# An audio block of mixer, mLSTM and eight experts on one core: a shorter router and last norm, and one expert pair of each of nine output blocks stored ahead

## The chip, the cores and the metric

The kernel runs on one core of one Trainium2 chip. The metric is the device time of one execution in microseconds (us), lower being better. All arithmetic is in float32.

## The reference

`x` is [64, 4, 256] and the output [64, 256, 64] (batch, token, feature). Three sub-blocks follow one another:

```python
# token mixer: 8 rounds in both directions, then a combination
a = x^T W1 + b1;  up = down = 0
for _ in range(8):
    up   = relu(a + shift_r(up) @ W2.T + b2)
    down = relu(a + shift_l(down) @ W2.T + b2)
h = relu(x^T W3 + b3 + shift_r(up) @ W4.T + b4 + shift_l(down) @ W4.T + b4)
# gated recurrence over 256 tokens (mLSTM) on layernorm(h), then an RMS norm
h = h + rmsnorm(mlstm(layernorm(h))) * norm_scale
# eight experts on z = layernorm(h), weighted per token
feat = mean(z, axis=0)                       # over the 64 batch elements
w = softmax(feat @ Wr + br)                  # [256, 8]
e = relu(bn(z @ W1[e] + b1)); e = relu(bn(e @ W2[e] + b2)); y = e @ Wo[e] + bo
out = h + sum_e w[:, e] * y[:, :, e]
```

The router's weights `w` depend on the mean over all batch elements, so no expert output can be weighted before the last batch element has been normalised. The first two layers of an expert don't depend on `w`.

## The kernel before, in words

The 64 batch elements are eight groups of eight. A half of a group is a tile of 128 partitions by 512 columns (two batch elements of 64 features on the partitions, two more side by side in the columns). `turn(it, ...)` exists on every engine and runs three stages of different groups interleaved by hand: the mixer of group `it`, the recurrence of group `it - 1` (`att`), and the `late` part of group `it - 2`: the RMS norm, the update of `HH` (the residual stream), and the norm whose result is kept in `XN2`. Turns 0 to 7 have a mixer; turn 8 has the recurrence of group 7 and the late part of group 6; turn 9 has only the late part of group 7. Engines work through their own lists in order and meet at semaphores.

The late part in turn 9: ACT squares `HR` (L538), PE averages (`same_half`, L781), DVE adds (L1212), ACT takes logarithm and exponential (L596, L600), POOL multiplies (`RSL`, L414), DVE updates `HH` (L1246), PE centres (`center`, L774), ACT squares (L617), PE averages (L951), ACT takes logarithm and exponential (L634, L637), DVE multiplies into `XN2` (L1297), POOL adds four slices of it into `feat` (L434).

Work ahead: `ahead_step(i)` computes the first two layers of expert pair `i` before the router is known. The experts are four pairs (EP = 4), and the activations 16 output blocks `F` of 512 columns (512 x 128), so there are 64 tasks `t`, with block `t // 4` and pair `t % 4`. Seven tasks, t = 0 to 6, are stored in `H2_AHEAD`: steps 0 to 4 in turn 8, 5 and 6 in turn 9, and the second layer of task 6 behind it. PE does `experts_in` (L848) and `experts_mid` (L856), ACT both activations (L487, L493).

Behind turn 9, DVE works out whether the decays are out of range (`wide_f`, L1363 to L1374), with a PE transpose between (L1023), and sets `wide_ready`. Then every engine reads this flag (`plain_pass`, L260: `value_load` at L263) and jumps past a long alternative pass that these inputs don't need.

The router: PE multiplies `feat` by `wr` and adds `br_row` (L1035, L1036); DVE and ACT make the softmax (L1380 to L1388); DVE spreads each weight over 64 columns (`wb`, L1391); PE turns this with 16 matmul records into the weight planes (L1043), and transposes `wn` (L1047); DVE copies the planes into `WM[0]` (L1394), ACT and DVE make the half-swapped `WM[1]` (L688, L1399). `bias_out` (L1051) makes the experts' bias per token, which DVE copies to `BOW` (L1433).

The expert stream: PE's loop (L1089) issues for each `t` the first layer of `t` (`l1`), the second layer of `t - 1` (`l2`) and the third of `t - 2` (`l3`, L1079). ACT does the first activation (L694), DVE the second one together with the weight (`weigh`, L1412). Stored tasks are weighed from SBUF, others from PSUM. The four third layers of a block add up in QB0 and QB1; then DVE adds the residual (`finish`, L1420, L1422) from the tile that POOL made (L462), transposes it (`token_major`, L1427), and SP stores it (L335). DVE's order is t = 0, 1, 2, ..., with `finish` behind the first weighing of the next block, and `token_major` behind the second. The next block's first third layer (`l3` with p = 0) waits for `finish` (semaphore `res`).

Of the kernel before, what the change touches and what calls it, by code (L numbers as in the profile page):

```python
# [42 lines left out]
def build(nc, x, tok_W1, tok_b1, tok_W2, tok_b2, tok_W3, tok_b3, tok_W4, tok_b4, Wq, bq, Wk, bk, Wv, bv,  # L43
          Wg, bg, input_bias, norm_scale, Wr, br, W1, b1, g1, be1, m1, v1, W2, b2, g2, be2, m2, v2, Wo, bo, out):
    with ExitStack() as ctx:
# [26 lines left out]
        col2 = sb("col2", [P, 8])  # L72
        bn_s = sb("bn_s", [P, 2, EP])
# [37 lines left out]
        V0 = sb("V0", [P, HC])  # L111
        UT0 = sb("UT0", [P, HC])
# [14 lines left out]
        bn_rows = SQL[0:NBN, P:2 * P]  # L127
        w2_raw = RSL[:, 0:P]
# [13 lines left out]
        wb = NN[:, :].rearrange("p (t c) -> p t c", t=2)  # L142
        wn = M[:, 0:16].rearrange("p (t e) -> p t e", t=2)
        wx = M[:, 16:32].rearrange("p (t e) -> p t e", t=2)
        wmx, wsm, wrc = M[:, 32:34], M[:, 34:36], M[:, 36:38]
        wt = Q[0:E, 0:T]
# [6 lines left out]
        QB = [ctx.enter_context(nc.psum_tensor(f"QB{j}", [P, 512], F32)) for j in range(4)]  # L153
# [33 lines left out]
        def bn_cols(name):  # L187
# [45 lines left out]
            "lg_mm", "mx", "nmx", "ex", "rc", "wn", "wb", "w_mm", "w_out", "wt_mm", "wt_out", "bo_mm", "bo_out",  # L233
            "ws_out", "l1_mm", "h1", "l2_mm", "h2", "hw", "l3_mm", "res_a", "res", "tr_out")}
        stored = [sem("b_stored0"), sem("b_stored1")]
# [6 lines left out]
        range_max, range_mm, range_all, wide_ready = (sem(n) for n in ("range_max", "range_mm", "range_all", "wide_ready"))  # L242
        feat_cleared, fold_mm, range_parts = sem("feat_cleared"), sem("fold_mm"), sem("range_parts")
# [6 lines left out]
        def settle(engine, it, mix, att, late):  # L250

            if mix:
                engine.wait_ge(s["feat_out"], SB * it)
            if att:
                engine.wait_ge(s["h1_a"], it)
                engine.wait_ge(s["h1_v"], it)
            if late:
                engine.wait_ge(s["hr_out"], 2 * it - 2)

        def plain_pass(engine, turn, prepare=None, again=None):  # L260
# [3 lines left out]
            with engine.If(wide != 0):  # L264
# [6 lines left out]
                engine.wait_ge(s["feat_out"], 2 * SB * G)  # L271
# [4 lines left out]
        N_AHEAD = 2 * EP - 1  # L276
# [12 lines left out]
        def _(sp):  # L289
# [34 lines left out]
            with sp.If(wide != 0):  # L324
                with sp.Fori(0, G) as g:
# [5 lines left out]
            with sp.Fori(0, G) as g:  # L331
                for f in range(2):
                    sp.wait_ge(b["tr_out"], 2 * g + f + 1)
                    for q in range(4):
                        sp.dma_start(ov[bass.ds(g, 1), q // 2, q % 2, f].rearrange("a i n b j -> (a i) n b j"),  # L335
                                     OUTT[f][32 * q:32 * q + 32, :].rearrange("i (n b j) -> i n b j", n=2, j=32))\
                            .then_inc(stored[f], 16)
            for f in range(2):
                sp.wait_ge(stored[f], 64 * G)

        @block.gpsimd
        def _(pool):
# [63 lines left out]
            def turn(it, att, late, plain=False):  # L406
                a, l = it - 1, it - 2
                gl = l - G if plain else l
                if plain:
                    settle(pool, it, False, att, late)  # L410
                if late:
# [18 lines left out]
                if late:  # L430
                    for n in range(SB):
                        pool.wait_ge(s["xn2_out"], 2 * l + n // 2 + 1)
                        pool.wait_ge(s["feat_out"], SB * l + n)
# [7 lines left out]
            turn(G + 1, False, True)  # L441
# [5 lines left out]
            def clear_feat():  # L447
                pool.wait_ge(s["feat_out"], SB * G)
# [5 lines left out]
                pool.wait_ge(feat_cleared, 4)  # L454

            plain_pass(pool, plain_turn, clear_feat)

# [8 lines left out]
        def _(act):  # L466
# [15 lines left out]
            def ahead_step(i, done=0):  # L482

                if i < N_AHEAD:
                    for k in range(2):
                        act.wait_ge(ahead["l1_mm"], 2 * (done + i) + k + 1)
                        nc.scalar.activation(H1[i % 2][:, k, :], TB[k][:, :], ACT.Relu,  # L487
                                             bias=bn_t[:, 0, i % EP:i % EP + 1]).then_inc(ahead["h1"], 1)
                if i > 0:
                    j = i - 1  # L490
                    for k in range(2):
                        act.wait_ge(ahead["l2_mm"], 2 * (done + j) + k + 1)
# [976 lines left out]
```

## Time and profile before

| | us |
|---|---|
| median of three timed runs | 651.35 |
| lowest, highest | 648.98, 654.53 |
| the profiled execution, whole | 656.66 |
| its span in the trace | 654.9 |
| its mean granted TensorE clock | 0.95 |
| busy in the span: PE, DVE, ACT, POOL | 594.1, 438.4, 343.4, 128.8 |

The profile is of one execution. PE is the TensorE matmul, PEld its weight load, DVE VectorE, ACT ScalarE, POOL GpSimd, SP SyncE. A granted clock of 1.00 is 2.4 GHz, 0.50 is 1.2 GHz. Matmul durations of one instruction overlap, since four matmuls of 64 by 64 go side by side; start-to-start times and the chain give the pace. L12 is line 12 of the kernel before.

### The profile page before, as it was taken

Reading aid. Unit: us, or ns where it says so; the run is one execution under the profiler, and the core shown is the slowest. Engines: PE = TensorE matmul, PEld = TensorE weight load, DVE = VectorE, ACT = ScalarE, POOL = GpSimd, SP = SyncE. Lnnn points to the kernel's source line nnn. Section 1 sums busy time; section 2 is a strip of 40 time slices with the busy share of each in tenths; the row PEclk is TensorE's granted clock in tenths of the full one; section 3 lists DMA queues with packets and bytes.
Section 4 is the critical chain, followed back from the end, with each engine's and each line's share of the span. In section 5 each row is a group of like instructions: output and inputs, shape, how many; then the busy total and the mean of one; then the engine's idle time right before and its main releaser. Section 6 shows DMA issues by size and latency. Waiting matters only on the chain.

```text
span 654.9 us, 11761 instructions
## 1 busy us (share of the span) xinstructions
PE 594.1 (91%) x4715; PEld 231.9 (35%) x4715; DVE 438.4 (67%) x742; ACT 343.4 (52%) x609; POOL 128.8 (20%) x145
## 2 busy tenths in 40 slices
PE   7889898999999999999999999786479999999995
PEld 5233342344334334334334334342323333333331
DVE  2335864893895895894795794782277767676765
ACT  1237352854845845845845846965213444444441
POOL 9100020132113113113113113242220101010100
PEclk8999996989999999989999989997579999999998
DMA  1300000000000000000000000000002121212122
GB/s 41 87 3 2 1 3 0 1 2 3 2 1 3 2 1 4 0 2 5 1 0 2 1 1 2 0 1 1 6 2 33 17 33 17 35 18 33 17 33 33
DMA packets 37433, 7.29 MB, mean 11 GB/s; under 512 B 36405, under 2 KB 36701, under 8 KB 37373
## 3 DMA queue, kind: packets, MB, share of 16 engines
q1 hardware_dynamic: 36301, 5.72, 5.1%
q8 instruction: 40, 0.66, 0.4%
q0 software_dynamic: 768, 0.69, 0.4%
q14 instruction: 20, 0.16, 0.1%
q10 hardware_dynamic: 304, 0.07, 0.0%
HBM read 2.26 MB, written 4.19 MB: 10 GB/s over the span
## 4 chain that ended last, share of the span: by engine, by line
PE 73%; DVE 18%; issue 4%; ACT 3%; POOL 1%; POOLq 0%; DVEq 0%
PE TB L731 14%; PE TB L721 9%; PE QB L1079 7%; PE QB L754 6%; PE TB L848 6%; PE QB L781 5%; PE TB L856 4%; DVE M L1241 3%; PE QB L774 3%; PE TB L829 3%; PE QB L856 2%; PE TB L781 2%; DVE E L1412 2%; PE QB L798 2%; DVE XC_IS L1422 2%
## 5 line engine op out<-in xcount | busy, mean ns | idle before, releaser
L479 ACT ACTIVATE U<-TB 128x512 f32<-128x512 f32 x128 | 69.5, 596 | 135.1 <-PE TB L721 135.1
L731 PE MATMUL TB<-U,w2T 64*64 64x512 f32 x896 | 130.4, 618 | 8.6 <-ACT U L479 4.7
L694 ACT ACTIVATE E<-TB,bn_t 128x512 f32<-128x512 f32 x114 | 72.1, 683 | 95.5 <-PE TB L848 95.5
L1123 DVE TENSOR_SCALAR U<-TB 128x512 f32<-128x512 f32 x128 | 82.0, 683 | 57.5 <-PE TB L721 57.5
L721 PE MATMUL TB<-X,w_in 6*128 6x512 f32 x512 | 74.0, 648 | 2.1 <-DVE fw L1355 0.9
L848 PE MATMUL TB<-XN,fw 64*64 64x512 f32 x512 | 69.6, 605 | 1.2 <-DVE AT L1394 0.9
L731 PEld LDWEIGHTS TB<-U,w2T 64*64 64x64 f32 x896 | 43.8, 136 | 67.1 <-issue 30.1
L1079 PE MATMUL QB<-E,fwo 64*64 64x512 f32 x240 | 63.2, 598 | 4.1 <-DVE XC_IS L1422 3.5
L1079 PE MATMUL QB<-E,fwo_sw 64*64 64x512 f32 x240 | 62.4, 598 | 0.0
L1412 DVE SCALAR_TENSOR_TENSOR E<-TB,t_neg,AT 128x512 f32<-128x512 f32 x56 | 39.5, 747 | 29.8 <-PE TB L856 29.8
L754 PE MATMUL QB<-XC_IS,wproj 64*64 64x512 f32 x384 | 56.5, 606 | 2.9 <-ACT LI L582 2.7
L414 POOL TENSOR_TENSOR RSL<-HR,RSL 128x512 f32<-128x512 f32 x16 | 20.9, 1328 | 179.6 <-ACT RSL L600 179.6
L1412 DVE SCALAR_TENSOR_TENSOR E<-QB,t_neg,AT 128x512 f32<-128x512 f32 x58 | 40.7, 744 | 16.9 <-PE QB L856 16.9
L462 POOL TENSOR_TENSOR SQ<-HH,LF_UT 128x512 f32<-128x512 f32 x16 | 21.2, 1329 | 146.3 <-DVE XC_IS L1420 126.5
L422 POOL TENSOR_TENSOR IK<-NN,M 128x512 f32<-128x512 f32 x16 | 20.1, 1275 | 147.5 <-DVE NN L1278 147.5
L856 PE MATMUL TB<-E,fw 64*64 64x512 f32 x280 | 39.1, 615 | 0.2 <-ACT E L493 0.2
L774 PE MATMUL QB<-HH,center_mat 64*64 64x512 f32 x128 | 25.6, 749 | 14.8 <-DVE AT L1129 9.7
L721 PEld LDWEIGHTS TB<-X,w_in 6*128 6x128 f32 x512 | 20.2, 185 | 51.4 <-issue 48.2
L848 PEld LDWEIGHTS TB<-XN,fw 64*64 64x64 f32 x512 | 20.0, 135 | 36.3 <-ACT E L694 25.7
L798 PEld LDWEIGHTS QB<-Q,K 64*128 64x128 f32 x256 | 23.2, 198 | 26.2 <-issue 13.4
L798 PE MATMUL QB<-Q,K 64*128 64x256 f32 (+1 forms) x256 | 29.2, 359 | 3.1 <-DVE AT L1129 3.1
L1079 PEld LDWEIGHTS QB<-E,fwo 64*64 64x64 f32 x240 | 16.7, 134 | 42.6 <-issue 24.6
(218 smaller groups left out, 918.7 us busy)
## 6 DMA issues: line engine op xcount, KB each, us to landing
result<-V SPq DMA_DIRECT2D x64, 64.0 KB, 1.8
X<-in_x SPq DMA_DIRECT2D x32, 8.0 KB
XN<-in_ffn_v SPq DMA_DIRECT2D x2, 256.0 KB, 4.3
XN<-in_ffn_g SPq DMA_DIRECT2D x2, 256.0 KB, 4.7
fw<-in_ffn_W POOLq DMA_DIRECT2D x2, 128.0 KB, 2.9
fw<-in_ffn_W POOLq DMA_DIRECT2D x2, 64.0 KB, 2.6
fwo<-in_ffn_Wo POOLq DMA_DIRECT2D x2, 64.0 KB, 2.3
fwo_sw<-in_ffn_Wo POOLq DMA_DIRECT2D x2, 64.0 KB, 2.3
```

The costliest lines, as they stand in the source:

```text
L479: nc.scalar.activation(U3[:, 2 * j:2 * j + 2, 1:T + 1], rowsof(TB[j][:, :]), ACT.Relu)\
L694: nc.scalar.activation(H1[t % 2][:, k, :], TB[k][:, :], ACT.Relu, bias=bn_t[:, 0, t % EP:t % EP + 1]).then_inc(b["h1"], 1)
L721: pe.matmul(TB[j][:, :], w_in[32 * j:32 * j + KA, 0:P], X[32 * j:32 * j + KA, buf, :], start=(k == 0), stop=True).then_inc(s["mix_mm"], 1)
L731: pe.matmul(TB[j][half[r ^ (j % 2)], :], w2T[half[r], D * r:D * r + D], U3[half[r], 2 * j:2 * j + 2, 2 * down:2 * down + T], start=True, s ...
L754: mm = pe.matmul(bank[half[r ^ h], :], wproj[half[r], PROJ[p], :], XC_IS[half[r], hs(h)], start=True, stop=True)
L781: mm = pe.matmul(bank[half[r], :], mat[half[r], D * r:D * r + D], src[half[r], :], start=True, stop=True)
L798: mm = pe.matmul(bank[:, T * c:T * c + w], K[half[k], f:f + C], Q[half[k], f:f + w], start=True, stop=True)
L848: mm = pe.matmul(banks[k][half[e], :], fw1[half[r], t % EP, D * e:D * e + D], XN2[half[r], HC * F:HC * F + HC], start=True, stop=True)
L856: mm = pe.matmul(banks[k][half[e ^ k], :], fw2[half[e], t % EP, D * e:D * e + D], H1[t % 2][half[e], k, :], start=True, stop=True)
L1079: mm = pe.matmul(QB[r][half[k], :], (fwo, fwo_sw)[k][half[r], p, :], src[half[r], k, :], start=(p == 0), stop=(p == EP - 1))
L1123: nc.vector.tensor_scalar(U3[:, 2 * j:2 * j + 2, 1:T + 1], rowsof(TB[j][:, :]), 0.0, None, ALU.max)\
L1412: nc.vector.scalar_tensor_tensor(out=rowsof(v[:, k, :]), in0=rowsof(bank[k] if bank else v[:, k, :]), scalar=t2_neg[:, k, t % EP:t % EP + ...
```

## The change

- *Which tasks are stored.* `stored` is now t = 0, 4, 8, ..., 32, the first pair of each of nine blocks: eight by `ahead_step` (N_AHEAD = 8) and the ninth, t = 32, "parked": its layers are issued on PE around the logits, and ACT stores it. Their buffers are others (`X`, both parts of `U`, `K`, `NC_`, `LI`, `decay0` and so on). `made` lists the tasks whose layers run in the stream, with t = 32 first.
- *Who stores.* ACT does the second activation for stored tasks 0 to 5 and 7, DVE for task 6 (`ON_DVE` = 6). In turn 9, pair 5 keeps its place, pair 6 goes before the third list of projections (behind `rms_mm`), pair 7 to the place that pair 6 had, and the last second layer behind turn 9 as before.
- *Late part of turn 9.* The products of L414 move from POOL to DVE. The last multiplies into `XN2` move behind `plain_pass` on DVE. POOL's four last adds into `feat` are left out; PE adds group 7 in the logits instead, four slices by `wr`, two matmuls each.
- *Range check.* `range_parted` moves into turn 8 on DVE, the transpose to PE's start of turn 9, the rest to DVE's turn 9 ahead of the products.
- *Router.* One instruction for both token halves; no spreading over 64 columns. `wn` is written four times, 32 columns apart, so that two transposes put the weights at partitions 0, 32, 64, 96, and eight matmuls with a constant `pick` matrix (8 rows each) make all planes of `WM`, half-swapped ones included. DVE and ACT copy half of the planes each.
- *Order.* `weigh_order` weighs a stored t > 0 before t - 1. In PE's loop a stored task's third layer is issued directly ahead of its successor's. `finish` and `token_major` come one weighing later where the block's first task is stored.

The core of the diff ("..." where lines are left out):

```diff
-        H2_AHEAD = [E3[:, :], E2[:, 1024:2048], U[:, 0:1024], K[:, :], H2_4[:, :], RS_FS[:, :], E2[:, 0:1024]]
+        H2_AHEAD = [E3[:, :], H2_4[:, :], X[:, :, :].rearrange("p a c -> p (a c)"), U[:, 0:PC], U[:, PC:2 * PC], K[:, :],
+                    NC_[:, :], LI[:, :], decay0[:, :, :].rearrange("p n t -> p (n t)"), IK[:, :], V0_UT0[:, :], EO[:, :]]
         H2_AHEAD = [v.rearrange("p (s c) -> p s c", s=2) for v in H2_AHEAD]
         WM = [AT[:, 0:4, 0:T], AT[:, 4:8, 0:T]]
+        WM_BY_PAIR = AT[:, :, 0:T].rearrange("p (v j) c -> p j v c", v=2)
...
-        N_AHEAD = 2 * EP - 1
+        N_AHEAD, N_PARKED, ON_DVE = 8, 1, 6
+        stored = [EP * i for i in range(N_AHEAD + N_PARKED)]
+        stored_in = {t: H2_AHEAD[i] for i, t in enumerate(stored)}
+        made = stored[N_AHEAD:] + [t for t in range(2 * EP * G) if t not in stored_in]
+        weigh_order = sorted(range(2 * EP * G), key=lambda t: t - 1.5 if t in stored_in and t > 0 else t)
+        weighed = {t: 2 * i + 2 for i, t in enumerate(weigh_order)}
...
-                if late:
+                if late and not last_late:
...
-                if late:
+                if late and gl < G - 1:
...
+            h1(0)
+            act.wait_ge(b["nmx"], 1)
+            nc.scalar.activation(wx, wx, ACT.Exp).then_inc(b["ex"], 1)
+
+            park(0)
+            h1(1)
+            act.wait_ge(b["w_mm"], 1)
+            nc.scalar.activation(WM_BY_PAIR[:, 2:4], QBALL[:, 1024:2048].rearrange("p (j v c) -> p j v c", j=2, v=2),
+                                 ACT.Identity).then_inc(b["ws_out"], 1)
+
+            for i in range(N_PARKED + 1, len(made)):
+                h1(i)
...
                 if last_late:
+                    pe.wait_ge(range_max, 1)
+                    pe.wait_ge(s["den_sq"], 2 * G - 1)
+                    pe.transpose(QB[0][0:1, 0:P], wide_f[:, 0:1], ident[:, :]).then_inc(range_mm, 1)
...
-            l1(N_AHEAD)
+            l1(0)
+            pe.wait_ge(s["feat_out"], SB * (G - 1))
+            pe.wait_ge(wide_ready, 1)
+            pe.wait_ge(s["den_sq"], 2 * G)
+            for t in range(2):
+                pe.matmul(QB[t][:, 0:E], ones_row[:, :], br_row[:, :], start=True, stop=False)
+                pe.matmul(QB[t][:, 0:E], feat[:, P * t:P * t + P], wr[:, :], start=False, stop=False)
+            for n in range(SB):
+                pe.wait_ge(b["xn2_last"], n // 2 + 1)
+                for t in range(2):
+                    o = (G - 1) * PC + T * n + P * t
+                    mm = pe.matmul(QB[t][:, 0:E], XN2[:, o:o + P], wr[:, :], start=False, stop=(n == SB - 1))
+                    if n == SB - 1:
+                        mm.then_inc(b["lg_mm"], 1)
+            l2(0)
+
+            pe.wait_ge(b["wn"], 1)
+            for t in range(2):
+                mm = pe.transpose(QB[3][:, P * t:P * t + P], wn[:, t, :, :].rearrange("p j r -> p (j r)"), ident[:, :])
+            mm.then_inc(b["wt_mm"], 1)
+            l1(1)
+            pe.wait_ge(b["wt_out"], 1)
+            pe.wait_ge(pick_ready, 5)
+            for v in range(2):
+                for j in range(EP):
+                    mm = pe.matmul(QB[j][:, T * v:T * v + T], pick[32 * j:32 * j + E, D * v:D * v + P], wt[32 * j:32 * j + E, :],
+                                   start=True, stop=True)
+            mm.then_inc(b["w_mm"], 1)
+
+            l2(1)
+            l1(2)
             bias_out()
-            for t in range(N_AHEAD - 1):
+            n = len(made)
+            for i in range(N_PARKED + 2, n + 2):
+                if i < n:
+                    l1(i)
+                if i - 1 < n:
+                    l2(i - 1)
+                t = made[i - 2]
+                if t - 1 in stored_in:
+                    l3(t - 1)
                 l3(t)
...
+                if last_late:
+                    for e in range(2):
+                        nc.vector.tensor_reduce(pick_col[:, e:e + 1], ident[:, e:e + 103:34], AX_X, ALU.add).then_inc(pick_ready, 1)
+                    dve.wait_ge(pick_ready, 2)
+                    for i in range(3):
+                        nc.vector.tensor_copy(pick[:, D * i:D * i + D], pick_col[:, i % 2:i % 2 + 1].to_broadcast([P, D]))\
+                            .then_inc(pick_ready, 1)
+                    range_check()
+                    for h in range(2):
+                        dve.wait_ge(s["rr_out"], 2 * l + h + 1)
+                        nc.vector.tensor_tensor(RSL[:, hs(h)], HR[:, hs(h)], RSL[:, hs(h)], ALU.mult).then_inc(s["y_out"], 1)
...
+            for h in range(2):
+                dve.wait_ge(s["rs2_out"], 2 * G - 1 + h)
+                nc.vector.tensor_tensor(xn2(G - 1, h), hh(G - 1, h), RSL[:, hs(h)], ALU.mult).then_inc(b["xn2_last"], 1)
+            dve.wait_ge(b["wn_cleared"], 1)
+            lg = QBALL[:, 0:1024].rearrange("p (t c) -> p t c", t=2)[:, :, 0:E]
+            dve.wait_ge(b["lg_mm"], 2)
+            nc.vector.tensor_reduce(wmx, lg, AX_X, ALU.max).then_inc(b["mx"], 1)
+            dve.wait_ge(b["mx"], 1)
+            nc.vector.tensor_tensor(wx, lg, wmx.unsqueeze(2).to_broadcast([P, 2, E]), ALU.subtract).then_inc(b["nmx"], 1)
+            dve.wait_ge(b["ex"], 1)
+            nc.vector.tensor_reduce(wsm, wx, AX_X, ALU.add).then_inc(b["sm"], 1)
+            dve.wait_ge(b["sm"], 1)
             nc.vector.reciprocal(wrc, wsm).then_inc(b["rc"], 1)
             dve.wait_ge(b["rc"], 1)
-            for t in range(2):
-                nc.vector.tensor_scalar(wn[:, t, :], wx[:, t, :], wrc[:, t:t + 1], None, ALU.mult)\
-                    .then_inc(b["wn"], 1)
-            for t in range(2):
-                dve.wait_ge(b["wn"], t + 1)
-                nc.vector.tensor_copy(wb[:, t, :].rearrange("p (e c) -> p e c", c=D),
-                                      wn[:, t, :].unsqueeze(2).to_broadcast([P, E, D])).then_inc(b["wb"], 1)
+            nc.vector.tensor_tensor(wn[:, :, :, 0:E], wx.unsqueeze(2).to_broadcast([P, 2, EP, E]),
+                                    wrc.unsqueeze(2).unsqueeze(3).to_broadcast([P, 2, EP, E]), ALU.mult).then_inc(b["wn"], 1)
+            dve.wait_ge(b["wt_mm"], 1)
+            nc.vector.tensor_copy(wt, QB[3][:, 0:T]).then_inc(b["wt_out"], 1)
...
-            for t in range(2 * EP):
+            for t in weigh_order:
+                if t == 2:
+                    dve.wait_ge(b["ws_out"], 1)
                 weigh(t)
-                if t == 1:
+                if t == 0:
                     dve.wait_ge(b["bo_mm"], 1)
                     nc.vector.tensor_copy(BOW, QB[3][:, 0:T]).then_inc(b["bo_out"], 1)
-                if t == EP:
-                    finish(0)
-                if t == EP + 1:
-                    token_major(0)
-            for t in range(2 * EP, 2 * EP * G):
-                weigh(t)
-                if t % EP == 0:
-                    finish(t // EP - 1)
-                if t % EP == 1:
-                    token_major(t // EP - 1)
+                F, behind = t // EP - 1, t % EP - (t - t % EP in stored_in)
+                if F >= 0 and behind == 0:
+                    finish(F)
+                if F >= 0 and behind == 1:
+                    token_major(F)
```

`bias_out`, `l1`, `l2` and `l3` do what they did. `l2` for the second task of `made` beyond the parked one waits for `bo_out`, since it writes the bank of the bias.

## Rows read from the trace of the kernel before

**Rows 1.** The page, busy time and share of the span.

```profile
PE 594.1 (91%) x4715; PEld 231.9 (35%) x4715; DVE 438.4 (67%) x742; ACT 343.4 (52%) x609; POOL 128.8 (20%) x145
```

**Rows 2.** Stretches: from:to, length, busy by engine (instructions), PEclk, DMA share, GB/s.

```profile
120.00:390.00 270.00, 261.24 (x2091) 104.53 (x2085) 209.53 (x353) 168.49 (x309) 58.43 (x53) 0.98 0.01 2
...
455.00:470.00 15.00, 7.00 (x35) 3.30 (x27) 2.80 (x12) 6.21 (x14) 3.27 (x4) 0.61 0.02 6
470.00:480.00 10.00, 7.95 (x30) 5.05 (x31) 6.12 (x12) 2.41 (x4) 0.00 (x0) 0.50 0.01 2
480.00:490.00 10.00, 7.38 (x40) 2.92 (x38) 6.93 (x9) 0.00 (x0) 3.39 (x2) 0.82 0.00 0
```

**Rows 3.** The chain that ended last, hand-over: start, length, what.

```profile
447.94 1.27 POOL RSL L414
...
449.24 1.74 DVE HH L1246
...
451.03 2.63 PE QB L774 x8
...
459.40 0.70 DVE XN L1297
...
463.89 3.02 issue
466.90 0.56 PE QB L1035 x2
...
469.08 0.18 DVE M L1380
...
471.16 3.77 PE TB L1043 x16
...
474.95 1.24 DVE AT L1394
```

**Rows 4.** The same chain from the first layer to the last transpose.

```profile
476.23 1.99 PE TB L848 x8
...
479.37 3.73 PE QB L1056 x8
...
501.46 1.09 PE QB L1079 x8
502.55 0.86 PE TB L848 x8
...
512.24 1.09 PE QB L1079 x8
...
641.56 1.09 PE QB L1079 x8
...
650.19 0.71 DVE V L1427
```

**Rows 5.** PE's sequencer at line 263, the flag: durations in ns, start in us.

```profile
L263 PEldq TENSOR_LOAD <-wide_i x1: 492/492/492, 462.3 to 462.3; - x1
...
L263 PEldq SEQ_ASSERT  x1: 24/24/24, 463.1 to 463.1; - x1
```

**Rows 6.** Stretches of 2 us, columns as in rows 2 (granted clock third from last).

```profile
446.00:448.00 2.00, 0.00 (x0) 0.00 (x0) 0.68 (x1) 1.87 (x5) 0.06 (x1) 1.00 0.00 0
450.00:452.00 2.00, 0.97 (x6) 0.60 (x10) 1.64 (x2) 0.00 (x0) 0.43 (x1) 0.50 0.00 0
456.00:458.00 2.00, 1.58 (x14) 0.49 (x6) 0.00 (x0) 2.00 (x5) 0.00 (x0) 0.94 0.00 0
458.00:460.00 2.00, 0.00 (x0) 0.00 (x0) 0.60 (x1) 1.89 (x4) 0.00 (x0) 0.92 0.00 0
482.00:484.00 2.00, 2.00 (x11) 0.79 (x13) 0.89 (x2) 0.00 (x0) 0.38 (x1) 0.61 0.00 0
```

**Rows 7.** Groups of the weighing, from SBUF (beside POOL) and from PSUM.

```profile
L1412 DVE SCALAR_TENSOR_TENSOR K<-K,t_neg,AT 128x512 f32<-128x512 f32 x2 | 2.4, 1248 | 0.0
...
L1412 DVE SCALAR_TENSOR_TENSOR E<-TB,t_neg,AT 128x512 f32<-128x512 f32 x56 | 39.5, 747 | 29.8 <-PE TB L856 29.8
```

More of the change, by code:

```diff
@@ L408, in turn @@
                 gl = l - G if plain else l
+                last_late = it == G + 1 and not plain
                 if plain:
                     settle(pool, it, False, att, late)
-                if late:
+                if late and not last_late:
                     for h in range(2):
@@ L480, in relu, with ahead_h1, ahead_h2, ahead_again @@
                         .then_inc(s["relu_a"], 1)
-            def ahead_step(i, done=0):
-                if i < N_AHEAD:
[L485 to L492, printed above, removed]
-                        nc.scalar.activation(H2_AHEAD[j][:, k, :], TB[2 + k][:, :], ACT.Relu,
-                                             bias=t2_pos[:, k, j % EP:j % EP + 1]).then_inc(ahead["h2"], 1)
+            def ahead_h1(i, done=0):
+                p = stored[i] % EP
+                for k in range(2):
+                    act.wait_ge(ahead["l1_mm"], 2 * (done + i) + k + 1)
+                    nc.scalar.activation(H1[i % 2][:, k, :], TB[k][:, :], ACT.Relu,
+                                         bias=bn_t[:, 0, p:p + 1]).then_inc(ahead["h1"], 1)
+            def ahead_h2(i, done=0):
+                p = stored[i] % EP
+                for k in range(2):
+                    act.wait_ge(ahead["l2_mm"], 2 * (done + i) + k + 1)
+                    nc.scalar.activation(H2_AHEAD[i][:, k, :], TB[2 + k][:, :], ACT.Relu,
+                                         bias=t2_pos[:, k, p:p + 1]).then_inc(ahead["h2"], 1)
+            def ahead_again(i, done):
+                if i < N_AHEAD:
+                    ahead_h1(i, done)
+                if 0 < i <= ON_DVE or i == N_AHEAD:
+                    ahead_h2(i - 1, done)
             def att_plain(a, g):
@@ L851, in experts_in, with experts_mid @@
                             mm.then_inc(done, 1)
-            def experts_mid(t, banks, done):
+            def experts_mid(t, hidden, banks, done):
                 for k in range(2):
@@ L856, in experts_mid @@
                         mm = pe.matmul(banks[k][half[e ^ k], :], fw2[half[e], t % EP, D * e:D * e + D],
-                                       H1[t % 2][half[e], k, :], start=True, stop=True)
+                                       hidden[half[e], k, :], start=True, stop=True)
                     mm.then_inc(done, 1)
@@ L863, in ahead_step @@
                     after(pe, ahead["h1"], 2 * (done + i))
-                    experts_in(i, TB[0:2], ahead["l1_mm"])
+                    experts_in(stored[i], TB[0:2], ahead["l1_mm"])
                 if i > 0:
@@ L1124, in relu, with ahead_h2, ahead_again @@
                         .then_inc(s["relu_v"], 1)
+            def ahead_h2(i, done=0):
+                p = stored[i] % EP
+                for k in range(2):
+                    dve.wait_ge(ahead["l2_mm"], 2 * (done + i) + k + 1)
+                    nc.vector.tensor_scalar(H2_AHEAD[i][:, k, :], TB[2 + k][:, :], t2_pos[:, k, p:p + 1], 0.0, ALU.add, ALU.max)\
+                        .then_inc(ahead["h2"], 1)
+            def ahead_again(i, done):
+                if ON_DVE < i < N_AHEAD:
+                    ahead_h2(i - 1, done)
             def scores(a, bs):
@@ L1184, in turn @@
                 gm, ga, gl = (it - G, a - G, l - G) if plain else (it, a, l)
+                last = it == G and not plain
+                last_late = it == G + 1 and not plain
                 if plain:
@@ L1293, in turn @@
                     relu(it, 7)
-                if late:
+                if late and gl < G - 1:
                     for h in range(2):
@@ L1297, in turn @@
                         nc.vector.tensor_tensor(xn2(gl, h), hh(gl, h), RSL[:, hs(h)], ALU.mult).then_inc(s["xn2_out"], 1)
+                if last_late:
+                    dve.wait_ge(s["lam_out"], G)
+                    for i in range(6, N_AHEAD - 1):
+                        ahead_h2(i)
+                if last:
+                    range_parted()
                 if mix:
```

223 lines of the change are left out of this document (108 added, 115 removed).

## The prediction

> **What bounds the kernel now.** I read the page's busy shares first: PE is busy for 91% of the span [rows 1]. The stretches by stage say where the rest is. In the eight-group body (120 to 390 us) PE is busy 261 of 270 us; but between 455 and 490 us it has 22.3 busy us in 35, at a granted clock of 0.61, 0.50 and 0.82 [rows 2]. So there are three regimes: a body that the change hardly touches, a hand-over of some 45 us bound by a serial chain at half clock, and a stream of expert blocks that PE bounds.
>
> The chain of waits shows the hand-over [rows 3]. POOL's product of the last group's late half starts at 447.94; DVE's update of HH beside it takes 1.74 us, and PE has nothing to do until the centring at 451.03. The multiplies of the last norm begin at 459.40, POOL then adds four slices into feat, and 3.02 us of "issue" follow: PE has taken the jump past the unused plain pass (the flag is read at 462.3, the last of its instructions starts at 463.1 [rows 5]) and issues its first router matmul only at 466.90, 3.7 us after the jump. The logits end at 469.05, the softmax runs to 471.1, the broadcast matmuls take 3.77 us and the copy of the weights 1.24 us. Then one first layer (1.99 us at half clock), the bias matmuls to 483.1, and the stream [rows 4]. A step (a first, second or third layer of one pair, 8 matmul records) takes 0.86 us at full clock; a block of four pairs is 12 steps and lasts 10.78 us (501.46 to 512.24), so about 0.46 us go to waiting for the finish of the block before.
>
> The clock by 2 us slices [rows 6]: PE does nothing from 446 until 451.03 and is at 0.50 afterwards; with matmuls going since 451.03 the clock is back within 456 to 458; it falls again in 458 to 460, when PE has run out of work, and stays at 0.50 through router and bias until 482 to 484, though wide matmuls had restarted at 476.23.
>
> **The change part by part.** All in the profiled execution's own time.
>
> *Body.* Same matmuls. Only the destinations of stored pairs differ, and range arithmetic moves into turn 8, where DVE waits. Cost 0; if the wait didn't cover it, under 1 us.
>
> *Turn 9.* PE does the range transpose before pair 5 (about 0.2 us), and DVE makes the pick matrix and reads the range before the products: about ten small operations of some 0.15 us, beside ACT's logarithm and exponential (446.7 to 447.9). I charge 0.15 us. The two products on DVE take 0.70 us each, as the nearest row (459.40), so HH's first update again begins near 449.4, but with POOL silent I take 0.70 instead of 1.74 us: centring starts at about 450.2, 0.8 us earlier. Pair 6 of the work ahead now fills 446.0 to 447.8, so PE idles 2.4 instead of 5.2 us, and I take it to keep full clock. Centring then takes 1.1 instead of 2.6 us, and pair 7's first layer and pair 6's second halve too. ACT loses two second-layer copies to DVE. Adding up: centring to 451.9, squares to 452.6, variance to 454.5, logarithm and exponential to 456.8 (459.9 before). Bounds: 0 to 4 us earlier; I take 3.
>
> *The jump.* It was behind the last norm; now wide_ready is early and the order on each engine decides. PE issues pair 7's second layer when DVE has stored pair 6 (about 455.1), reads the flag at 455.7, has read it at 456.5, and by the same 3.7 us starts at 460.2. Bounds: 2 us (another engine's load out of the way) to 4.6. DVE does its jump before the last norm multiplies: flag at 453.9, free at about 458.4, multiplies done at 459.8. PE and DVE thus hide the jump behind each other; it is PE's that is on the path. POOL's adds go from it.
>
> *Router.* PE idles 4 us ahead of it, so I take half clock: first layer of pair 32, 2.0 us, to 462.2. Logits are now 12 matmuls, 24 records, instead of 8: in the chain the 8 records took 2.15 us, 0.27 each, so 6.4 us, to 468.6. This is the added cost that eats most of POOL's adds. Softmax: one maximum, subtract, exponential, sum, reciprocal, product, each some 0.2 us: 1.4 us, hidden by second layer of pair 32 (2.0, to 470.6), which PE has queued ahead of the transposes. Two transposes at 0.24 per record [rows 3]: 0.5, plus a start of 0.1, to 471.2. The first layer of pair 1 (2.0, to 473.2) hides DVE's copy of 256 columns (0.4). The eight selecting matmuls (8 rows, 256 columns) have no row. The nearest is the bias: 3.73 us for four of 128 by 256 [rows 4], so 7.5 us one by one at half clock, 0.9 at full clock with four side by side in their row strips. They are laid out in four strips like the kernel's input matmuls, so I take 1.6: 474.8. The first two weight planes are copied by DVE, the others by ACT, 1.24 us each beside one another and beside second layer 1 and first layer 2.
>
> *Clock and bias.* Wide matmuls go on without a gap from 468.6. The two restarts shown took 5 to 7 us to bring the clock back [rows 6]; so I take full clock from about 474. Two steps (1.7) lead to 476.5, bias at full clock 2.45, to 479.0 against 483.1. Bounds: 484 (half clock to the end of the bias) to 472 (no fall at all).
>
> *Stream.* Nine pairs' first two layers and two more first layers lie before the bias; 171 steps remain instead of 177. Blocks: the first 12 steps and a wait, 10.8; eight with a stored pair, 10.78 minus two steps, 9.06 each, 72.5; six as before, 64.7; the last from 641.56 to 650.90, 9.3 [rows 4]. Together 157.3 us. Before it was 167.8 us from bias to end, because six stored pairs in a row waited for DVE, first at 2.4 us per pair, and let the clock fall again at 490 to 494. End at 479.0 + 157.3 = 636.3, against 650.9: 14.6 us earlier.
>
> *DVE in a stored block* has four weighings of 1.41, two additions of 0.69 and a transpose of 0.70: 7.7 of 9.06 us, and the stored one is done while second layers are still coming. What can break that is a row: a weighing out of SBUF took 1.25 us per half beside POOL's product, one out of PSUM 0.75 [rows 7]. POOL's residual sum starts at the finish and lasts 1.3 us; DVE then weighs from PSUM, and the stored pair comes 2 us later, so I charge 0. The upper bound is 1.1 us per block, 8.8 us.
>
> The Trainium skill (SBUF — State Buffer, "SBUF: two separate sides") says that a VectorE operation with two SBUF inputs and a GpSimd one that reads SBUF lock each other out for a whole instruction. The stored weighing has two SBUF inputs. If that met POOL in every block, the rule would bring the upper bound just named, and the trace's 1.25 against 0.75 us agrees with it.
>
> **The rivals.** *A. The clock never falls* (the 4 us gap is bridged, as a 2.4 us one is): logits 3.3, steps 0.86; bias ends at 472, end at 629.3, 21.6 us gained. For it: denser work before the gap. Against: 459 to 460, where it fell about 2 us after the last matmul. *B. Half clock to the end of the bias*, as before from 462 to 482: bias ends at 484, end at 641.4, 9.5 us gained. *C. DVE bounds stored blocks* through the port: 14.6 minus up to 8.8, about 8 us gained. *D, slower:* the clock does not return once the stream runs: each step then costs 2.0 instead of 0.86 us, 1.14 more. From 13 slow steps beyond the bias the gain is gone, if bias is slow too from 9; three blocks at half clock (30 steps, 34 us) make it 20 to 25 us slower. Against it stands every restart in this trace, none longer than about 7 us, and the full clock in all steady blocks. *E. It does not do what it says:* the second bank pair waits for the bias copy and stored pairs stall DVE as now. Then only the 6 steps and the turn's 3 us are gained, about 8 us; the first block's order, with at most one stored pair at a time, speaks against it.
>
> **How the numbers follow.** Forecast 0.50; A 0.14; B 0.18; C and E 0.13 together; D 0.03; 0.02 for what none of them names. The profiled execution took 656.66 us (span 654.9), 5.3 above the median of 651.35. The forecast is 656.66 − 14.6 = 642.1 in its time, 0.978 of it; against the median 651.35 × 0.978 = 636.9. A gives 629.9, B 641.9, C and E 643.4. The range takes in all of these and the jump's bounds: 628.5 to 644. One per cent, 6.5 us, is about what a measurement of this kernel can tell. Faster by over 1% is 0.92 (all but D, the rest, and a part of C and E), within it 0.05, slower 0.03.
>
> **What would show it.** Right: centring near 450 with clock 1.00; last multiplies about 458 to 460; first PE work after the flag 3.7 us behind it; logits of 24 records over some 6 us at clock 0.50; bias ending at 478 to 480; blocks of 9.06 us eight times, then 10.78; no idle PE over 1 us after the bias. Wrong: logits at 1.00 (A), bias at 0.50 (B), stored weighings of 1.2 us per half or blocks over 9.5 us (C), slices of 0.50 after 485 (D), gaps between third layers in the first two blocks (E). A first PE instruction that comes much sooner or later than 3.7 us after the flag would make the jump's term wrong.

## The result and the profile after

The changed kernel takes 634.28 us (median of five, 633.63 to 636.97) against 652.43 us of the kernel before in the same session (648.98 to 654.65): ratio 0.9736, 95% interval 0.9697 to 0.9775, some 18 us. The forecast was 637 us, ratio 0.978, and "faster"; 0.978 stands just above the interval's upper end. Its profiled execution has a span of 635.2 us and a mean granted clock of 0.967.

The page, where rows 1 were:

```profile
PE 587.7 (93%) x4731; PEld 229.5 (36%) x4731; DVE 436.5 (69%) x747; ACT 344.4 (54%) x608; POOL 123.1 (19%) x140
```

A float32 matmul leaves two records in the trace. The chain through the hand-over, answering to [rows 3, 4] (start, length, what; "issue" is time for which the profile shows nothing that the engine waited for):

```profile
442.99 1.29 DVE RSL L1354 x2
444.28 0.68 DVE HH L1358
...
445.00 1.31 PE QB L819 x6
...
449.46 1.09 PE TB L901 x8
450.55 3.60 issue
454.15 1.99 PE TB L893 x8
...
457.71 0.53 PE QB L1128 x2
458.23 3.41 PE QB L1133 x16
461.64 1.92 PE TB L901 x8
463.56 0.62 PE QB L1140 x2
464.18 1.92 PE TB L893 x8
466.09 2.02 PE QB L1147 x16
468.11 1.92 PE TB L901 x8
470.03 1.41 PE TB L893 x8
...
472.06 1.92 PE QB L1086 x8
...
484.69 1.95 PE QB L1117 x16
...
493.75 1.95 PE QB L1117 x16
```

HH's update is 0.68 us where it was 1.74; no POOL step stands in the chain; the 3.60 us of issue are PE's jump. From 454.15 PE works without a hole: the parked pair's first layer, the logits (L1127 to L1133, 5.5 us), the parked pair's second layer, transposes, planes (L1147), bias. From one stored block to the next it is 9.06 us. The clock (columns as in rows 2):

```profile
454.00:456.00 2.00, 1.85 (x8) 0.31 (x8) 0.00 (x0) 0.00 (x0) 0.00 (x0) 0.50 0.06 16
...
466.00:468.00 2.00, 2.00 (x20) 1.22 (x16) 0.00 (x0) 1.27 (x2) 0.00 (x0) 0.50 0.00 0
470.00:472.00 2.00, 2.00 (x15) 0.36 (x7) 0.85 (x2) 0.50 (x1) 0.00 (x0) 0.75 0.00 0
472.00:474.00 2.00, 2.00 (x13) 1.51 (x16) 0.00 (x0) 0.76 (x2) 0.00 (x0) 1.00 0.00 0
```

At 0.50 from the jump to about 471, at 1.00 for the bias (L1086: 1.92 us where it was 3.73) and all that follows. Stored pairs weighed from SBUF in the stream cost 0.72 to 0.74 us per half, not 1.25 (groups of 484 to 563 us; the first row is from PSUM, for comparison):

```profile
L1516 DVE SCALAR_TENSOR_TENSOR E<-TB,t_neg,AT 128x512 f32<-128x512 f32 x27 | 19.0, 744 | 9.2 <-PE TB L901 9.2
...
L1516 DVE SCALAR_TENSOR_TENSOR K<-K,t_neg,AT 128x512 f32<-128x512 f32 x2 | 1.4, 729 | 0.0
```

### The profile page after: what moved, and what is told of

The parts are those of the page before. It is cut to its first block, busy times and chain, and to the rows that moved or that the text cites. A ratio compares the mean times of both kernels' runs of the same rounds, so it can differ in the third digit from the quotient of the medians.

```text
span 635.2 us, 11790 instructions
## 1 busy us (share of the span) xinstructions
PE 587.7 (93%) x4731; PEld 229.5 (36%) x4731; DVE 436.5 (69%) x747; ACT 344.4 (54%) x608; POOL 123.1 (19%) x140
## 4 chain that ended last, share of the span: by engine, by line
PE 76%; DVE 16%; issue 4%; ACT 3%; POOL 0%; DVEq 0%; POOLq 0%
PE TB L776 15%; PE TB L766 10%; PE QB L1117 7%; PE QB L799 7%; PE TB L893 6%; PE QB L826 5%; DVE M L1342 4%; PE TB L901 3%; PE QB L901 3%; PE QB L819 3%; PE TB L874 3%; PE QB L843 2%; DVE E L1516 2%; PE TB L826 2%; DVE XC_IS L1526 2%
## 5 line engine op out<-in xcount | busy, mean ns | idle before, releaser
L893 PE MATMUL TB<-XN,fw 64*64 64x512 f32 x512 | 71.2, 611 | 4.0 <-issue 3.6
L1117 PE MATMUL QB<-E,fwo 64*64 64x512 f32 x224 | 58.4, 593 | 2.3 <-DVE XC_IS L1526 1.7
L1117 PE MATMUL QB<-E,fwo_sw 64*64 64x512 f32 x224 | 57.6, 593 | 0.0
L1516 DVE SCALAR_TENSOR_TENSOR E<-QB,t_neg,AT 128x512 f32<-128x512 f32 x54 | 38.0, 745 | 21.9 <-PE QB L901 21.9
L430 POOL TENSOR_TENSOR RSL<-HR,RSL 128x512 f32<-128x512 f32 x14 | 18.5, 1339 | 173.2 <-ACT RSL L629 173.2
L901 PE MATMUL TB<-E,fw 64*64 64x512 f32 x296 | 42.2, 617 | 0.3 <-ACT H L513 0.2
L819 PE MATMUL QB<-HH,center_mat 64*64 64x512 f32 x128 | 22.3, 635 | 12.0 <-DVE AT L1211 9.7
L1211 DVE TENSOR_TENSOR AT<-QB,causal 128x384 f32<-128x384 f32 x64 | 31.5, 540 | 0.0
```

The lines of the kernel that those rows point to most:

```text
L893: mm = pe.matmul(banks[k][half[e], :], fw1[half[r], t % EP, D * e:D * e + D], XN2[half[r], HC * F:HC * F + HC], start=True, stop=True)
L901: mm = pe.matmul(banks[k][half[e ^ k], :], fw2[half[e], t % EP, D * e:D * e + D], hidden[half[e], k, :], start=True, stop=True)
L1117: mm = pe.matmul(QB[r][half[k], :], (fwo, fwo_sw)[k][half[r], p, :], src[half[r], k, :], start=(p == 0), stop=(p == EP - 1))
L1516: nc.vector.scalar_tensor_tensor(out=rowsof(v[:, k, :]), in0=rowsof(bank[k] if bank else v[:, k, :]), scalar=t2_neg[:, k, t % EP:t % EP + ...
```

## The experiments

To compare profiles whose starts scatter, each is divided at two points: *A* is from the start of the last mixer matmul of group 7 (`w_in` with 7 rows), called the cut below, to the first full bias matmul (of 128 rows), *B* from there to the start of the last transpose. *A* thus holds the hand-over, *B* the bias and the stream. Each *A* and *B* is of one profiled execution, each ratio of five or six timed ones. Ratios are to the kernel before, timed on the same chip.

| run | ratio, interval | A, us | B, us |
|---|---|---|---|
| before (profile above) | 1 | 80.8 | 170.9 |
| before_again | | 80.5 | 170.4 |
| after | 0.9736, 0.9697 to 0.9775 | 78.6 | 158.4 |
| after_again | 0.9742, 0.9709 to 0.9774 | 75.9 | 158.4 |
| stride_only | 0.9921, 0.9895 to 0.9947 | 80.6 | 166.5 |
| contig | 0.9870, 0.9839 to 0.9901 | 78.6 | 167.6 |
| no_park | 0.9813, 0.9768 to 0.9858 | 76.9 | 162.5 |
| pool_products | 0.9773, 0.9732 to 0.9813 | 79.3 | 158.5 |
| no_jump | 0.9667, 0.9640 to 0.9694 | 69.0 | 158.5 |
| filler | 0.9686, 0.9647 to 0.9726 | 75.6 | 158.5 |
| pool_adds | 0.9684, 0.9657 to 0.9712 | 75.1 | 158.6 |
| filler_pool | 0.9668, 0.9641 to 0.9694 | 72.2 | 158.5 |
| filler_pool2 | 0.9668, 0.9629 to 0.9706 | 71.4 | 158.5 |

**Both kernels again.**

> The kernel before, unchanged, for a second profile. The two profiled executions differ by 19.7 us in span, but from the last mixer input of group 7 (398.0 us before, 392.9 after) to the last transpose they differ by 14.7. Theory: the 5.1 us ahead of that point are scatter of this kernel's start and of its clock in the first turns; a second profile of before then has that point anywhere between 392 and 399 us, and the remainder within 1 us of 252.9. Rival: the change makes the body itself 5 us shorter; then the point lies at 398 again.

> The changed kernel, unchanged. Ratio 0.974 by every theory. Scatter theory: the last mixer input of group 7 moves by some us against 392.9, and from there to the last transpose it is 238.2 within 1 us. Body theory: the point stays at 393.

The second profiles, of the kernel before and of the changed one, at their mixer's last matmuls (first and last start at the end of the first part):

```profile
L838 PE MATMUL TB<-X,w_in x64: 587/613/638, 39.3 to 393.1; 7*64 7x512 f32 x64
```

```profile
L883 PE MATMUL TB<-X,w_in x64: 587/613/639, 39.7 to 393.2; 7*64 7x512 f32 x64
```

The kernel before reaches the point at 393.1 as well as at 398.5, so the 5 us of the first pair of profiles are scatter: none of the twelve other profiles is later than 394.9. The changed kernel's cut stayed at 393, but it is the kernel before that decides, and its cut moved. The granted clock moved with it: in 10 to 20 us it was 0.83 in the first profile before and 1.00 in the second, in 80 to 120 us 0.87 and 0.91. In *B* both kernels repeat within 0.5 us. In *A* the changed kernel doesn't: 75.9 against 78.6, a miss of the expectation (within 1 us), since the clock was back to 0.85 in 464 to 466 in the second profile and only at 471 in the first. By profile the gain is thus 2 to 5 us in *A* and 12 in *B*.

**The stride alone added (stride_only, on the kernel before), the stride alone undone (contig).** stride_only also takes the changed kernel's buffers for its seven tasks. All edits from contig on are on the changed kernel. "..." stands for lines left out.

```diff
         N_AHEAD = 2 * EP - 1
+        stored_t = [EP * i for i in range(N_AHEAD)]
...
+        weigh_order = sorted(range(2 * EP * G), key=lambda t: t - 1.5 if t in stored_in and t > 0 else t)
```

> The kernel before with the stride alone: seven stored tasks as before, but t = 0, 4, ..., 24, and the new order of weighing and of third layers; late part, router, range check and jump as before. Same 177 steps behind the bias. Theory (the stalls of the first blocks go): bias end where it was, stream 162.4 instead of 167.8 us, so 5.4 us faster, ratio 0.992. Rival (the stored tasks' weighings meet POOL's sum and DVE bounds their blocks): blocks of about 10.8 instead of 9.06 us, nothing gained, ratio 1.00.

```diff
-        stored = [EP * i for i in range(N_AHEAD + N_PARKED)]
+        stored = list(range(N_AHEAD + N_PARKED))
...
+        weigh_order = list(range(2 * EP * G))
...
+            for t in range(N_AHEAD):
+                l3(t)
...
```

> The changed kernel with the stride alone undone: tasks 0 to 8 stored, weighed in plain order, third layers of 0 to 7 issued at once behind the bias as in the kernel before. Same steps. Theory: DVE's weighings (1.4 to 2.5 us per stored task against 0.86 us for a third layer) hold PE up for 5 to 9 us, and the clock may fall once more there: 5 to 10 us slower than the changed kernel, ratio to before 0.982 to 0.989. Rival (stride is worth nothing, only the six steps and the hand-over count): 0.974 as the changed kernel.

stride_only gains 5.3 us in time (647.53 against 652.86, by the interval 3.5 to 6.9) for 5.4 forecast. By profile *B* is 3.9 to 4.4 us shorter than in the two profiles before, and *A* is as before; its blocks with a stored pair follow one another by 9.06 us (third layers at 492.17, 501.23, 510.29), which rules the rival (10.8) out. The chain of contig behind the bias:

```profile
474.49 1.92 DVE H L1518 x2
...
476.83 2.44 DVE X L1518 x2
...
479.31 3.74 PE QB L1117 x16
...
486.94 1.30 DVE NC_ L1518 x2
488.24 1.32 DVE LI L1518 x2
489.56 1.32 DVE decay L1518 x2
...
493.58 1.09 PE QB L1117 x8
```

Stored pairs that follow one another put DVE on the chain: of the 19.4 us between the bias and the first steady block (493.58) 3.74 are PE's and nearly all the rest DVE's. *B* is 9.2 us longer, the time 9.2 us (644.65 against 635.40 in the same session). Not all of that is DVE's own work. The clock fell in this stretch, as the expectation allowed:

```profile
480.00:482.00 2.00, 2.00 (x16) 0.45 (x8) 1.91 (x3) 0.00 (x0) 0.00 (x0) 0.50 0.00 0
```

The 16 third-layer records on the chain took 3.74 us, and 1.72 us in the changed kernel (start 475.86), so by these rows some 2.0 of the 9.2 us are the clock's. Three of the pairs (`H`, `X` and `K`) meet POOL's sums; here is `X`, as a group and by its two halves (shortest/median/longest in ns):

```profile
L1518 DVE SCALAR_TENSOR_TENSOR X<-X,t_neg,AT 128x512 f32<-128x512 f32 x2 | 2.4, 1250 | 0.0
```

```profile
L1518 DVE SCALAR_TENSOR_TENSOR X<-X,t_neg,AT x2: 740/1250/1760, 476.8 to 478.5; 128x512 f32<-128x512 f32 x2
```

So 1.25 us is a mean: one half took 1.76 us beside POOL's sum, the other 0.74, as the halves of pairs that met no sum did (0.70 to 0.74). POOL's two sums, from 474.66, took 3.39 us together, and 2.51 in the changed kernel. The Trainium skill (SBUF — State Buffer, "SBUF: two separate sides") says that a VectorE instruction with two SBUF inputs and a GpSimd one that reads SBUF shut each other out for a whole instruction; the trace agrees, since both engines were longer. In the changed kernel every stored pair in the stream escapes it: no half took more than 0.75 us.

**The ninth pair not parked.**

```diff
-        N_AHEAD, N_PARKED, ON_DVE = 8, 1, 6
+        N_AHEAD, N_PARKED, ON_DVE = 8, 0, 6
...
```

Ahead of the bias PE then has first layer, logits, transposes, first layer, planes, second layer; task 32 is made in the stream.

> The changed kernel without the ninth stored pair: N_PARKED = 0, task 32 is made in the stream, PE's list ahead of the bias is first layer, logits, transposes, first layer, planes, second layer. Theory: the stream has two steps more (1.7 us at full clock); ahead of the bias two steps at half clock go (3.9 us), but one of them hid the softmax (1.9 us) and the copies of the planes now stand against one second layer alone. Together between 0.5 us faster and 1.5 us slower than the changed kernel, ratio to before 0.973 to 0.976. Rival (the parked pair fills time that was idle): its two steps are worth their full 1.7 us and more, ratio 0.977 or more. Rival 2 (fewer wide matmuls ahead of the bias let the clock come back later): bias at 0.50, 0.978 or more.

Rival 2 came about: the bias ran at half clock.

```profile
472.00:474.00 2.00, 2.00 (x6) 1.64 (x5) 0.00 (x0) 0.00 (x0) 0.00 (x0) 0.50 0.00 0
476.00:478.00 2.00, 2.00 (x24) 0.76 (x20) 1.32 (x3) 1.26 (x2) 2.00 (x2) 0.98 0.00 0
```

*A* is 1.7 us shorter than in the first profile after, since two steps at half clock (3.8 us) are gone from it and 1.4 us of softmax, which one of them had hidden, stand on the chain (462.3 to 463.7); against the second profile it is 1.0 us longer. *B* is 4.1 us longer: 1.7 for two steps at full clock, 1.8 for the bias at half clock (3.71 against 1.92 us), the rest for the next first layer (1.49 against 1.02). In time the parked pair is worth 4 to 5 us (639.90 against 635.40 us in another session; the kernel before took 652.93 and 652.86), where I expected between -0.5 and 1.5, and every one of the six executions is longer than the longest of after_again. That two steps more of wide matmuls (512 columns) bring the clock back ahead of the bias is what one profile of no_park shows against two of the changed kernel.

**POOL's products back.**

```diff
-                if late and not last_late:
+                if late:
...
```

> The changed kernel with the two products of turn 9 back on POOL, ahead of DVE's updates of HH. Theory (port and clock): HH's first update takes 1.7 us again instead of 0.7, centring starts about 1 us later; PE's idle stretch ahead of it grows from 2.4 to 3.4 us, and if the clock stays at 1.00 the bias ends 1 to 1.5 us later: ratio to before 0.975 to 0.977. Rival (the clock falls in that stretch): centring at 0.50, 3 to 4 us later, ratio 0.979 to 0.980. Second rival (the jump hides it): same as the changed kernel, 0.974.

```profile
444.61 1.27 POOL RSL L430
...
445.91 1.75 DVE HH L1355
...
447.70 1.31 PE QB L819 x6
```

Centring starts 52.8 us behind the cut, in the changed kernel 51.6 (445.00 - 393.4). HH's update takes 1.75 us beside POOL's second product and 0.68 without it, as forecast. The clock was 1.00 over this gap, as over the smaller one, so the first rival is out. The products are worth 1.2 us by the profile. In time it is 3.1 us (638.51 against 635.40, another session); the ratio, 0.9773, stands just above the expectation (0.975 to 0.977), and its interval doesn't exclude the changed kernel's, so that the second rival (the jump hides it) isn't excluded by time.

**What the jump costs (no_jump), and what the clock costs (filler, four matmuls ahead of the jump).**

```diff
-            wide = engine.value_load(wide_i[:, :], min_val=0, max_val=1)
-            with engine.If(wide != 0):
...
```

> The changed kernel without the alternative pass and without reading the flag on any engine (these inputs never take that pass, and the flag is still computed). It prices the jump. In the changed kernel PE waits 3.6 us with nothing but issue between the last second layer ahead and the first layer of the parked pair, and the clock falls in it. Theory (jump and clock are one cost): the first layer follows within 0.2 us, last multiplies start on DVE at about 451.1, logits run at granted clock 1.00 in about 3.3 us, and the bias ends about 9 to 10 us sooner: ratio to before 0.958 to 0.961. Rival 1 (only the wait goes, the clock falls anyway or comes back at the same time): 3.6 us, ratio 0.969. Rival 2 (something else ends last, such as ACT's or DVE's part of the last norm): under 2 us, ratio 0.971 or more.

```diff
+N_FILL = 4
...
+            pe.wait_ge(s["den_sq"], 2 * G)
+            for _ in range(N_FILL):
+                pe.matmul(QB[1][:, :], center_mat[:, :], HH[:, 0:HC], start=True, stop=True)
```

> The changed kernel with four matmuls of 128 by 128 by 512 more (results unused) behind the last second layer ahead and in front of the flag: PE's array is busy for about 3.5 us while its sequencer jumps. The jump stays. Clock theory (what the jump costs beyond its wait is the clock, 0.50 from about 454 to 471 in the changed kernel): clock stays at 1.00, first layer 0.9 instead of 2.0 us, logits 3.3 instead of 5.5 and so on, bias end 6 to 8 us sooner, ratio to before 0.962 to 0.965. Rival 1 (router matmuls with 8 columns let the clock fall all the same): 1 to 4 us gained, 0.968 to 0.972. Rival 2 (the sequencer can't run ahead of the queued matmuls, so that the jump starts later by their 3.5 us): slower than the changed kernel, 0.976 or more.

The chain of filler, and its clock:

```profile
452.00 3.63 PE QB L1076 x8
455.63 1.02 PE TB L894 x8
...
457.92 1.96 PE QB L1137 x16
459.88 1.92 PE TB L902 x8
```

```profile
456.00:458.00 2.00, 2.00 (x19) 1.35 (x11) 0.00 (x0) 1.27 (x2) 0.00 (x0) 1.00 0.03 8
458.00:460.00 2.00, 2.00 (x20) 1.98 (x23) 0.01 (x1) 0.00 (x0) 0.00 (x0) 0.85 0.00 0
460.00:462.00 2.00, 2.00 (x10) 0.39 (x7) 0.90 (x5) 0.38 (x2) 0.00 (x0) 0.50 0.00 0
```

The filler bridges the jump: the sequencer jumps while the array works (rival 2 is out), the first layer takes 1.02 us, the 16 direct logit records 1.96 instead of 3.41. But within the logits the clock falls, although PE counts as busy for every moment, and it is back only behind 468. That is rival 1, and the ratio, 0.9686, is in its range too. The profile of no_jump shows the same: clock 0.99 in 454 to 456, and right behind the logits, which end at 455.92, 0.50:

```profile
456.00:458.00 2.00, 2.00 (x10) 0.38 (x6) 0.91 (x5) 0.43 (x2) 0.00 (x0) 0.50 0.00 0
```

This need not happen in every execution. The six of filler fall into two groups: 629.77 to 630.90 us at a mean granted clock of 0.981 to 0.983, and 633.86 to 637.15 at 0.970 to 0.976, the profiled one (635.47, 0.973) among these. The first three are as fast as the last version below, whose profile shows no fall (629.63 to 631.33 us, 0.981 to 0.984). No profile shows where their clock stood.

Without the jump *A* is 7 to 10 us shorter, the time 5 us (630.42 against 635.40; ratio 0.9667, nearer to the rival's 0.969 than to my 0.958 to 0.961). Part of the difference between the two is the choice of profile: that of no_jump is the fastest of its five executions, that of the first changed one the slowest, and the cut of no_jump lies 1.4 us later.

**POOL's adds instead of direct logits (16 records less on PE).**

```diff
+            for n in range(SB):
...
+                nc.gpsimd.tensor_tensor(feat[:, :], feat[:, :], XN2[:, (G - 1) * PC + T * n:(G - 1) * PC + T * n + T], ALU.add)\
+                    .then_inc(feat_last, 1)
...
-            for n in range(SB):
-                pe.wait_ge(b["xn2_last"], n // 2 + 1)
...
```

> The changed kernel with one part undone: POOL adds the last group's four slices into feat as before, and the logits are 8 matmul records instead of 24. In the changed kernel the last multiplies end at 453.5 and PE is free for the logits only at 456.1, so POOL's adds (0.8 us each, the first from 453.0) end at about 456.4, beside the jump and the first layer. Theory (the direct logits cost 16 records of 0.21 us and hide nothing here): logits end 3 us sooner, ratio to before 0.969. Rival (as the change assumes: POOL's chain is on the path): adds end at 457 or later and the softmax starts where it did or later, ratio 0.974 or more.

> Filler matmuls and POOL's adds together. Theory: with the clock at 1.00 the direct logits cost only about 2.1 us more than POOL's way, and the adds end later than PE's first layer (455), so that POOL's way gains 0 to 1.5 us on top of the filler alone: ratio 0.961 to 0.965. Rival (they add up in full): 0.957 to 0.960. Second rival: the wait for POOL, some 1.5 us without matmuls, lets the clock fall and gives the filler's gain back: 0.969.

pool_adds: logits end 64.8 us behind the cut instead of 68.2, ratio 0.9684 as the theory had it. This part of the change costs time, some 3 us (632.34 against 635.40, another session): POOL's four adds (453.12 to 456.76) run beside PE's jump and first layer and are done before PE has multiplied by `br_row` (457.24), and the matmuls that replace them are PE's own. With filler the ratio is 0.9668, short of the 0.961 to 0.965 expected; POOL's chain then ends last, PE idles 1.3 us and the clock falls again (0.50 in 460 to 462), which is half of the second rival. The last version adds two fillers there:

> The version with four filler matmuls in the jump and POOL's adds, and two more fillers of 128 by 128 by 512 between the parked pair's first layer and the wait for POOL's last add, where PE stood idle for 1.5 us and the clock fell at about 459.5. Theory (the clock fell for want of wide matmuls; the 8-column logits are now only 0.6 us): clock 1.00 from turn 9 to the end, bias end 1.5 to 2 us sooner than with four fillers, ratio to before 0.963 to 0.965. Rival (the softmax's chain with PE idle between is enough for the clock to fall): 0.967 as before.

```profile
455.05 0.54 PE QB L1138 x4
455.59 1.91 PE QB L1141 x4
457.50 0.36 PE QB L1144 x4
```

```profile
458.00:460.00 2.00, 1.56 (x14) 0.41 (x10) 1.09 (x6) 1.32 (x3) 0.00 (x0) 1.00 0.00 0
460.00:462.00 2.00, 1.83 (x24) 0.72 (x16) 0.30 (x2) 1.36 (x4) 0.00 (x0) 1.00 0.00 0
464.00:466.00 2.00, 2.00 (x12) 1.54 (x9) 0.58 (x1) 1.26 (x2) 0.00 (x0) 1.00 0.00 0
```

The clock is at 1.00 from turn 9 through the hand-over and in all of the stream, and *A* is the shortest with the jump in it, 71.4 us. By profile that is 0.8 us better than filler_pool, half of what I expected. The chains behind the logits say why, first filler_pool, then filler_pool2:

```profile
458.81 1.63 PE TB L910 x8
460.45 0.62 PE QB L1147 x2
```

```profile
457.95 0.18 DVE M L1497
...
459.30 0.44 PE QB L1150 x2
```

At half clock the parked pair's second layer (1.63 us) covers the softmax. At full clock it is done in 1.09 us, and the chain goes through the softmax, from 457.86, the end of the logits, to 459.30, 1.44 us. ACT's copy of the next first layer (1.26 us) is on the chain in both. The logits also end 0.3 us later from the cut, 64.7 against 64.3, since the two fillers take 1.91 us where PE waited 1.27 for POOL. In time the two versions can't be told apart (630.94 and 631.60 us), and the ratio, 0.9668, is the rival's 0.967, not the 0.963 to 0.965 of the theory whose clock came true. Every execution of both is shorter than every one of either kernel; they are 3.3% under the kernel before.

## Why the prediction was right, and where its sizes were off

The sign and mechanism held. Counted from the cut, the profile I argued from has the end of the last transpose at 252.4 us (650.9 - 398.5); I forecast 237.8 (636.3 - 398.5) and the first profile after shows 237.7 (631.1 - 393.4). That it fits to 0.1 us is luck, since the second shows 235.0. By its steps:

*Turn 9.* Centring forecast 0.8 us earlier, measured 0.9 from the cut; clock 1.00 as assumed. ACT's last exponential ended 3.8 us earlier from the cut (450.99, before 459.88), where I took 3 within 0 to 4. The multiplies behind it came 2.0 us earlier: DVE came out of its own jump only at 452.26. That cost nothing, because PE's jump ended later still, which was the step's own reading.

*The jump.* 3.7 us from the flag's check to PE's next matmul forecast, 3.8 measured (450.3 to 454.15; 3.60 of it stand as issue), 3.4 to 4.0 over the runs in which PE has nothing queued. PE's first layer began 60.8 us from the cut, 61.7 forecast.

*Router.* First layer 2.0 and 1.99. Logits 6.4 forecast, 5.5 measured: the 16 direct records take 0.21 us each, not 0.27. Softmax hidden by the parked pair's second layer, as said. Planes 1.6 forecast, 2.02 measured: four side by side, but wholly at half clock. Together the two make the router half a us shorter than forecast.

*Clock and bias.* Return 75.5 us from the cut forecast; measured about 77.6 and, in the second profile, 71. End of the bias 80.5 forecast, 80.6 and 77.9 measured. I took one time for what differs by 6 us between two profiles of one kernel; both ends of the bias lie within my bounds.

*Stream.* 157.3 forecast, 157.2 measured; eight blocks of 9.06, then 10.78. stride_only and contig confirm the stride by itself: 4 to 5 us with seven stored, 9 us with nine, 2.0 of these by the clock. The six steps fewer (6 × 0.86 = 5.2 us) no run took alone; no_park put two of them back, and its *B* fits their price. The 171 steps are right, their wording isn't: beside the nine stored pairs both layers of task 1 and the first of task 2 lie ahead of the bias, 21 steps of 192.

*The rivals.* C (port) and E (stalls stay) are excluded by 0.72 to 0.74 us per stored half and by the blocks. The 1.25 us of [rows 7], on which C stood, is a mean as in contig: one half of `K` took 1.76 us, the other 0.74. D never showed: the clock was 1.00 in 474 to 600 us. B happened in no_park. A needs more than a bridged gap: in their profiles filler and no_jump kept the clock until the logits and lost it there; filler_pool2 held it.

*The total.* The medians differ by 18 us (17.5 in the second session), 3 more than the 14.6 of the sum. Two measured differences can lie behind it: in the second profile the clock came back 6 us sooner than in the one that matches my sum, which made *A* 2.7 us shorter; and ahead of the cut the profiles of one kernel differ by up to 5.4 us. How the rest divides between these two in the timed runs, which have no profile, stays open. The term of the sum that was mis-sized is the clock's return in the hand-over.

## What to carry to other kernels

Spread work done ahead so that each piece meets the stream where its consumer has slack; in a row it put DVE on the chain here and cost 9.2 us. Price a jump over unused code with what each engine could have done meanwhile: POOL's adds were free beside PE's jump and first layer, and moving them onto PE, which ended last, cost some 3 us. Look at the granted clock behind a stretch of small matmuls also where PE is busy throughout: here it fell in or right behind 24 records of 8 columns (filler, no_jump), and held at 1.00 where eight such records stood between wide ones (filler_pool2).

## What the runs showed that I had not expected

TensorE's clock fell while the profile calls PE fully busy, which I had named only as a rival: in the profile of filler PE is busy for 2.00 us of 2 in 458 to 460, and the granted clock goes from 1.00 to 0.50 in that stretch while the logits, matmuls of 8 columns, run without a gap. The Trainium skill (TensorE: Matmul & The Clock Gate, "What's actually happening") says that the clock follows how busy the engine has been. Full busy time in the profile did not keep it at 1.00 here. That it was the few columns, and nothing else about these matmuls, no run shows, since none varied the columns alone.

Queued wide matmuls ran on while the sequencer jumped: eight records, 3.63 us in filler, filled the whole gap, and the first layer behind the jump followed without a wait.
